# Operands of the next attention group read in twenty small transfers instead of five large ones

## The reference

```python
Q = jnp.concatenate([Qc, Qr], axis=-1)          # 16 + 8 channels a head
K = jnp.concatenate([Kc, Kr], axis=-1)
scores = jnp.einsum('bhqd,bhkd->bhqk', Q, K)
scores = jnp.clip(scores, -80.0, 80.0)
scores = jnp.where(causal, scores, -jnp.inf)
weights = jax.nn.softmax(scores / jnp.sqrt(jnp.float32(d_qk)), axis=-1)
attn = jnp.einsum('bhqk,bhkd->bhqd', weights, V)
...
x = x + (attn @ W_O) * g                        # g: the gate, from the channel mix
```

## Time and profile before

| what | us |
|---|---|
| time, median of 3 runs (2309.99 to 2316.2) | 2314.51 |
| the profiled execution: time | 2312.27 |
| the profiled execution: span of the trace | 2310.5 |
| attention, first exponential to last (ScalarE) | 1096.05 to about 2222.7 |
| TensorE busy | 2043.6 (88%) |
| VectorE busy | 1712.0 (74%) |
| ScalarE busy | 1582.5 (68%) |

### The profile page before, as it was taken

How to read it: one execution, slowest core, us unless ns; L and a number is a source line. 1 busy time by engine, 2 the same in 40 slices (tenths; PEclk the granted TensorE clock), 3 DMA queues, 4 the chain that set the end, 5 groups by cost and what they waited for, 6 DMA issues and landing times. The chain is left out here.

```text
span 2310.5 us, 53758 instructions
## 1 busy us (share of the span) xinstructions
PE 2043.6 (88%) x23334; PEld 1033.8 (45%) x23334; DVE 1712.0 (74%) x2284; ACT 1582.5 (68%) x1833; POOL 639.1 (28%) x399
## 2 busy tenths in 40 slices
PE   5999999999986887877999898989998989888985
PEld 2656556565653555544333333333333333333344
DVE  7776675766649999995777777777777768777774
ACT  5545464554545555554989988988988989888951
POOL 2645455454546666664000000000000000000025
PEclk9999999999997989998999999999999999999997
DMA  3001001010114555556233213333123331133337
GB/s 95 19 19 38 19 19 37 19 37 19 57 36 129 140 172 143 167 153 184 50 70 75 51 34 75 70 70 76 37 57 70 70 70 45 46 70 84 106 102 259
DMA packets 124266, 178.56 MB, mean 77 GB/s; under 512 B 7424, under 2 KB 105472, under 8 KB 120192
## 3 DMA queue, kind: packets, MB, share of 16 engines
q1 hardware_dynamic: 122000, 172.89, 27.7%
q10 hardware_dynamic: 2032, 2.24, 0.3%
HBM read 91.21 MB, written 83.89 MB: 76 GB/s over the span
## 5 line engine op out<-in xcount | busy, mean ns | idle before, releaser
L1633 ACT ACTIVATE c_probs<-c_ps_b 128x1536 f32<-128x1536 f32 x544 | 853.8, 1569 | 0.0
L1745 PE MATMUL c_ps_o<-c_probs,c_v 128*32 128x256 f32 (+3 forms) x6656 | 603.2, 465 | 23.3 <-issue 19.5
L1665 DVE TENSOR_SCALAR c_probs<-c_probs 128x2048 f32<-128x2048 f32 (+2 forms) x415 | 433.9, 1055 | 148.3 <-ACT c_probs L1633 138.6
L1725 PE MATMUL c_ps_a<-c_qk 24*128 24x256 f16 (+2 forms) x2688 | 457.8, 298 | 58.8 <-ACT c_probs L1632 41.6
L1725 PE MATMUL c_ps_b<-c_qk 24*128 24x256 f16 (+2 forms) x8064 | 469.5, 301 | 28.8 <-issue 28.8
L1632 ACT ACTIVATE c_probs<-c_ps_a 128x512 f32<-128x512 f32 x544 | 385.6, 709 | 122.6 <-PE c_ps_o L1745 70.6
L1725 PEld LDWEIGHTS c_ps_a<-c_qk 24*128 24x128 f16 x2688 | 212.1, 94 | 428.8 <-issue 208.4
L1893 POOL TENSOR_TENSOR d_prod<-d_prod,d_x 128x1024 f32<-128x1024 f32 x12 | 38.2, 3199 | 1158.0 <-DVE d_prod L1881 1158.0
L1745 PEld LDWEIGHTS c_ps_o<-c_probs,c_v 128*32 128x32 f32 x6656 | 164.2, 110 | 272.5 <-issue 163.2
L258 POOL TENSOR_TENSOR a_hidh<-a_hid,a_hidh 128x512 f16<-128x512 f32 x128 | 170.0, 1346 | 233.7 <-ACT a_hidh L356 229.8
L1725 PEld LDWEIGHTS c_ps_b<-c_qk 24*128 24x128 f16 x8064 | 217.5, 95 | 31.6 <-issue 31.3
(11 more groups left out here) (245 smaller groups left out, 2908.5 us busy)
## 6 DMA issues: line engine op xcount, KB each, us to landing
c_qk<-qk_d SPq DMA_DIRECT2D x64, 384.0 KB
v_d<-b_val SPq DMA_DIRECT2D x16, 1024.0 KB
c_v<-v_d SPq DMA_DIRECT2D x16, 1024.0 KB
attn_d<-c_onorm SPq DMA_DIRECT2D x64, 256.0 KB, 2.1
rows<-in_x SPq DMA_DIRECT2D x16, 512.0 KB, 4.8
x_d<-rows_out SPq DMA_DIRECT2D x16, 512.0 KB, 3.2
rows<-x_d SPq DMA_DIRECT2D x16, 512.0 KB, 5.0
qk_d<-b_qc SPq DMA_DIRECT2D x64, 128.0 KB
```

Of the source, the lines that this page charges most:

```text
L1633: nc.scalar.activation(probs[:, t % NPROB, PARTS[1]], ps_b[:, t % 2], ACT.Exp, scale=unscale).then_inc(exp_b_done, 1)
L1665: nc.vector.tensor_scalar(tile, tile, P_MAX, P_MIN, ALU.min, ALU.max).then_inc(clip_done, 1)
L1725: mm = nc.tensor.matmul(into, k[rows, hk, kt * P:(kt + 1) * P], tokens[rows, hq], start=(i == 0), stop=(i == len(TERMS) - 1), tile_positio ...
L1745: mm = nc.tensor.matmul(ps_o[j * VW:(j + 1) * VW, column:column + w], v[:, kt, j * VW:(j + 1) * VW], probs[:, step % NPROB, j, at:at + w], ...
```

## The change

The operands of the next group are read in 20 transfers: for each head queries and keys, high and low half, 24 rows of 4 KB each (96 KB, 16 transfers), then the values in four parts of 128 rows of 2 KB (256 KB each). In attention SP now goes step by step: before step t's piece it waits until `qk_done` has reached t + 1, and issues one piece, in steps 4 to 23 of the group before. The slot is therefore filled one group later than before (group g + 1 during group g), once `pv_done` says that group g - 1 is finished. In the other even steps of a group (7 of them) one 128 KB piece of gates or x1 is read. All x1 blocks are in by then; the four attention rows are read in steps 4 to 7 of the last group. Group 0's operands are read by the projections with 20 transfers issued one behind the other.

```diff
-                        load_group(sp, d, first, 0, 0)
+                        for part in range(Operands.LOADS):
+                            load_group(sp, d, first, 0, 0, part)
...
-    LOADS = GH + 1
+    VPARTS = 4
+    LOADS = 4 * GH + VPARTS
...
-def load_group(sp, d, into, b, g):
-
-    for j in range(GH):
-        sp.dma_start(into.memory[VW * j:VW * j + D_QK], d["qk"][b, g * GH + j, 0:D_QK]).then_inc(into.loaded, 16)
-    sp.dma_start(into.v[:], d["v"][b, g]).then_inc(into.loaded, 16)
+def load_group(sp, d, into, b, g, part):
+
+    if part < 4 * GH:
+        j, kind, half = part // 4, part // 2 % 2, part % 2
+        sp.dma_start(into.memory[VW * j:VW * j + D_QK, kind, half], d["qk"][b, g * GH + j, 0:D_QK, kind, half]).then_inc(into.loaded, 16)
+    else:
+        n = KEYT // Operands.VPARTS
+        tiles = slice((part - 4 * GH) * n, (part - 4 * GH + 1) * n)
+        sp.dma_start(into.v[:, tiles], d["v"][b, g, :, tiles]).then_inc(into.loaded, 16)
...
+    STEPS = N // (BATCH * GROUPS)
...
-                load_group(sp, d, slots[1], 0, 1)
...
-                for group in range(BATCH * GROUPS):
-                    for c in range(CPB):
-                        store(group * CPB + c)
-                    if group + 2 < BATCH * GROUPS:
-                        load_group(sp, d, slots[group % 2], (group + 2) // GROUPS, (group + 2) % GROUPS)
-                        for n in range(NCH * group // (BATCH * GROUPS - 2), NCH * (group + 1) // (BATCH * GROUPS - 2)):
-                            sp.dma_start(ahead.gate[:, n], token_view(d["gate"])[n]).then_inc(ahead.gate_loaded, 16)
-                    if group == BATCH * GROUPS - 2:
-                        for n in range(ahead.X_ROWS):
-                            sp.dma_start(ahead.x1[:, n], token_view(d["x1"])[n]).then_inc(ahead.loaded[n], 16)
-
-                        for t in range(OUTS):
-                            sp.wait_ge(stored[t], 16 * (GROUPS * CPB // OUTS) + 16)
-                        for n in range(ahead.ROWS):
-                            for k in range(KT):
-                                sp.dma_start(ahead.attn[:, n, k], channel_view(d["attn"])[n, k]).then_inc(ahead.loaded[n], 16)
+                def load_rows(i):
+
+                    if i < NCH * TPC:
+                        n, j = i // TPC, i % TPC
+                        sp.dma_start(ahead.gate[:, n, j], token_view(d["gate"])[n, :, j]).then_inc(ahead.gate_loaded, 16)
+                    elif i < NCH * TPC + ahead.X_ROWS * TPC:
+                        n, j = (i - NCH * TPC) // TPC, i % TPC
+                        sp.dma_start(ahead.x1[:, n, j], token_view(d["x1"])[n, :, j]).then_inc(ahead.loaded[n], 16)
+
+                rows_loaded = 0
+                for t in range(N + LAG + 5):
+                    if t - LAG - 4 in end_at:
+                        store(end_at[t - LAG - 4])
+                    if t >= N:
+                        continue
+                    group, step = t // STEPS, t % STEPS
+                    sp.wait_ge(qk_done, t + 1)
+                    part = step - LAG - 1
+                    if group + 1 < BATCH * GROUPS and 0 <= part < Operands.LOADS:
+                        if part == 0 and group:
+                            sp.wait_ge(pv_done, group * STEPS)
+                        load_group(sp, d, slots[(group + 1) % 2], (group + 1) // GROUPS, (group + 1) % GROUPS, part)
+                    elif part < 0 or part >= Operands.LOADS:
+                        if step % 2 == 0:
+                            load_rows(rows_loaded)
+                            rows_loaded += 1
+                    if group == BATCH * GROUPS - 1 and 0 <= part < ahead.ROWS:
+                        if part == 0:
+                            for o in range(OUTS):
+                                sp.wait_ge(stored[o], 16 * (GROUPS * CPB // OUTS) + 16)
+                        for k in range(KT):
+                            sp.dma_start(ahead.attn[:, part, k], channel_view(d["attn"])[part, k]).then_inc(ahead.loaded[part], 16)
```

More of the change, by code:

```diff
@@ L1624, in _ @@
+                assert rows_loaded >= (NCH + ahead.X_ROWS) * TPC
             @block.scalar
@@ L1791, in layer1_output @@
         LOADS = 16 * (KT + 1)
+        early_rows = 16 * (TPC - 1)
         w_o, gate, loaded = scales.w_o, ahead.gate, ahead.loaded
@@ L1858, in _ @@
                 for n in range(NCH):
-                    act.wait_ge(loaded[n % SLOTS], LOADS * (n // SLOTS + 1))
+                    act.wait_ge(loaded[n % SLOTS], LOADS * (n // SLOTS + 1) + (early_rows if n % SLOTS < X_ROWS else 0))
                     if n >= HALVES:
@@ L1870, in low @@
                                                    ALU.mult, ALU.subtract).then_inc(t_low, 1)
-                dve.wait_ge(ahead.gate_loaded, 16 * NCH)
+                dve.wait_ge(ahead.gate_loaded, 16 * NCH * TPC)
                 low(0)
@@ L1890, in _ @@
                 for n in range(NCH - 1):
-                    pool.wait_ge(loaded[n % SLOTS], LOADS * (n // SLOTS + 1))
+                    pool.wait_ge(loaded[n % SLOTS], LOADS * (n // SLOTS + 1) + (early_rows if n % SLOTS < X_ROWS else 0))
                     pool.wait_ge(prod_done, n + 1)
```

## The result

The changed kernel takes **2226.8 us** (median of 4 runs, 2223.7 to 2230.5) against 2313.5 us of the kernel before (4 runs), a ratio of 0.9627 with a 95% interval of 0.9606 to 0.9647. The forecast was 2229 (2223 to 2250). The profiled execution took 2227.8 us with a span of 2226.1, 84.4 us shorter than before.

A forecast was written before the change was run, and what follows sets the result against it. ScalarE was taken to pace attention, with 83.5 us lost to stalls behind operand reads. Span 2310.5 - 83.5 + 1.5 - 1.3 + 0 = 2227.2, plus 1.8 outside it, gave 2229 us, range 2223 to 2250.

The forecast's parts named there:

- The 83.5 us behind the reads: Attention: stalls behind operand reads in 14 groups vanish when reads are spread; gain 83.5 us, bounds 62.6 to 83.5.
- The ruler of quiet half groups: Attention: ScalarE's gaps behind joined steps mark half groups; undisturbed ones take 32.47 us, 1006.57 for 31.
- The cause named, a fetch waiting behind reads: Attention: TensorE's instruction fetch on q8 waits behind operand reads, about 6.0 us in each of 14 groups.
- the third rival: Attention: the stall lies in TensorE's own stream, so only the start's gain comes; about 2312 us, chance 0.05.
- The reason given, packet size: Attention: 2 MB in 8 and 16 KB packets cost TensorE 6 us; much traffic in small packets costs nothing.
- the x1 burst: Attention: 4.38 MB around reads of x1 and attention rows, nearly all small packets, lengthened a half group by 0.1 us.
- a quarter of the stalls stays: Attention: lateness proportional to packet size leaves 20.9 of 83.5 us; 2250 us, chance 0.11.
- The cost of the pieces: Attention: small transfers cost 0.1 us for each of 15 groups reading operands; 1.5 us, bounds 0 to 3.1.
- The start of attention: First group: group 1's reads leave the start, so TensorE's wait there goes; gain 1.3 us, bounds 0 to 2.6.
- Projections: Group 0's 20 transfers take SP 8 to 10 us; cost 0, hidden by SP's waits, otherwise up to 6 to 8.
- Late operands: Group starts: TensorE waits for pieces arriving too late; 2569 us at 4 us each, chance 0.04 with other losses.

The follow-up runs named there:

- e6: Changed kernel plus useless bursts (four 384 KB reads, one 1024 KB) in large packets at steps 24 to 30 of groups 1 to 8; 2238.2 us.
- e9: Changed kernel plus eight useless large-packet bursts with a 1 KB-packet tail at step 5, operand pieces moved to steps 12 to 31; 2259.7 us.
- e2: Changed kernel, still spread over the steps, but operands read in five large transfers of 16 and 8 KB packets; 2229.9 us.
- e5: Changed kernel plus useless reads at step 25, a different kind and amount in each of several groups; 2230.7 us.
- e1: Kernel before with its own burst schedule, but operands cut into the 20 small transfers; 2253.7 us.
- e12: Changed kernel with five probability buffers instead of four and five x1 blocks read ahead instead of six; 2197.0 us.
- e4: Changed kernel with the operand pieces ten steps later, in steps 14 to 33; 2290.3 us.
- e8: Changed kernel plus eight useless large-packet bursts at steps 24 to 30, half the kernel before's operand amount in each; 2227.7 us.

## Why the prediction was right, point by point

- **The 83.5 us behind the reads.** Forecast gain 83.5, measured 1090.04 - 1006.60 = 83.44. The ruler of quiet half groups was exact, and the slow clock behind the stalls went with them, as assumed (88 us at the lower level before, none after). This term is nearly the whole sum.
- **The cause named, a fetch waiting behind reads.** Useless reads alone make q8 disappear and TensorE stand (e6, e9), and removing the density of the reads removes it (e2). This rules out the third rival (the burst is not the cause).
- **The reason given, packet size, was half the truth.** The prediction said that 2 MB in packets of 8 and 16 KB cost 6 us and small packets nothing. Large packets spread over the steps cost 0.1 us a group (e2), 1.9 MB of them at once cost 0.2 and then nothing (e5), and small packets in a burst still cost 1.9 (e1). What failed is the reading of the x1 burst as a proof that size alone decides. Packet size, amount and place all count (e1, e6 to e9); that they do so through what stands before the fetch when it falls due fits all runs, but is my reading of them. The number came out because the change also spreads the reads, and that alone is enough (e2). To that extent it was luck: had the change only cut the packets, the same reasoning would have promised nearly all of the 83.5 us, and 26.4 would have stayed.
- **The rival "a quarter of the stalls stays".** For the spread reads it did not come true: nothing stays. For small packets in a burst the ratio is 26.4 / 83.4 = 0.32, close to the quarter.
- **The cost of the pieces.** Taken as 1.5 us (0 to 3.1); nothing of it is seen, the 1006.60 us being 31 quiet half groups to within 0.1. The 0.1 us longer half groups are those of the last rows' reads and one other. The source of the term does not hold up either: the half group of 32.56 is the one that took 32.57 before, behind the reads of x1 and rows, and it is as long now that x1 is read elsewhere. So the 0.1 us can't be put down to the x1 burst.
- **The start of attention.** Forecast gain 1.3 (0 to 2.6); the first joined step comes 2.13 us earlier (1123.37 to 1121.24), of which 0.54 lie before the first exponential (1096.05 to 1095.51), leaving 1.6. One execution each says little here, but the other runs agree: from the first exponential to that joined step it is 26.9 to 27.3 us in the four traces with a burst at the barrier and 25.5 to 26.2 in the nine without (e12 apart), about 1.3 apart.
- **Projections.** SP spends 8.7 us on group 0's reads, as forecast (8 to 10), and nothing shows behind it: its last store of the stage even starts a little earlier, 1087.94 against 1089.08. The waits hid it.

```profile
1026.41 6.93 SPq L1478 DMA_DIRECT2D c_qk<-qk_d  x16
1033.38 1.77 SPq L1482 DMA_DIRECT2D c_v<-v_d  x4
...
1087.94 0.54 SPq L1053 DMA_DIRECT2D gate_d<-rows_out  x1
```

- **What the sum left out.** From the last joined step to the end of the span it is 98.3 us instead of 97.1, 1.2 us more; the sum had 0 there. In the runs of the experiments but e12 this stretch lies anywhere from 91.9 to 99.9 us, so the 1.2 are within what one execution differs from the next. In total: -2.1 - 83.4 + 1.2 = -84.4 us (2310.5 to 2226.1, rounded), against -83.3 forecast.
- **Late operands.** The room forecast was there; e4 shows what lies behind it.

## What to carry to other kernels

When an engine with a dense instruction stream stands still and the profile names no one it waits for, look at the instruction queue beside the data queues: if no packet comes on it while the data queues are near 100%, and the engine goes on right behind the next one, a late instruction fetch is the first suspect, and useless reads at a quiet place can test it. Here it helped not to issue several megabytes in one go: one transfer every few steps was enough even when it was 384 KB or 1 MB, and small packets softened a burst. Look at the granted clock behind the waits as well; it can be a good part of the loss. Before such a change, measure the rhythm of the undisturbed steps: it gives what can be won and names what comes next, here a buffer too few.

## What the runs showed of the hardware

- Behind a burst of 2.5 MB of operands and 0.5 MB of gates, issued within about 2.5 us, a 16 KB instruction fetch started 3.4 to 8.5 us late (estimated, 14 bursts of the kernel before). 1.9 MB in 16 KB packets, at step 25 of a group, cost 0.2 us and nothing (e5), but a burst of 1.25 MB at step 24 cost 4.7 (e8). I had expected the cost to rise from 1.5 MB on.
- The same 2.5 MB cost 12.8 us in sum over eight bursts in packets of 16 and 8 KB and 0.7 in packets of 1 KB; half of it in large packets cost 4.9, nearly all in one burst.
- TensorE's clock fell with long waits: in the kernel before 14 waits of 1.65 to 6.07 us went with 88 us at 1.2 GHz; in e6 the clock stayed at 2.4 GHz behind waits of up to 1.45 us and was at 1.2 GHz behind one of 3.05 us; in e1 it fell at a wait of 1.61 us and not at one of 2.28.
- Kernels with bursts differ more from execution to execution: the kernel before ran from 2300 to 2320 us over 17 runs, the kernel with later bursts from 2279 to 2298 over 8, the changed kernel from 2224 to 2231 over 4.
